# Layer 1 of a two-layer graph network: pairs of edge tiles, blocks of 42 nodes, and products of 126 or 128 rows and weight columns

## The chip, the cores and the metric

One core of one Trainium2 chip runs the whole program. The metric is the device time of one launch in microseconds (us), as the median of the runs shown. PE is TensorE's matrix unit, PEld its weight loads, DVE is VectorE, ACT is ScalarE, POOL is GpSimd, SP is SyncE.

## The reference, cut to what matters

There are 6250 nodes with 160 features (64 scalars, 32 vectors of 3) and 100,000 edges with `src` and `dst`; the edges are sorted by `dst`. Layer 0 passes messages and normalises; this change leaves its arithmetic alone. Layer 1 is:

```
h = relu(e10 @ W_fc1 / sqrt(10)) * sqrt(2);  w = h @ W_fc2 / 10      # per edge, 192 weights
y = node_linear(x)[src]                                               # per edge, 160 features
msg = (w0*y0, w1*y0) and (w2*y1, w3*y1), each times the four edge attributes a0..a3
agg = segment_sum(msg, dst)                                           # 16 edges a node on average
out = layernorm(x + self_part + a_node * (agg @ W_l2))
```

`a0` multiplies the scalar part and `a1..a3` are the components of the edge's direction: `w0*y0*a0` and `w2*y1*a0` keep their kind, `w1*y0*(a1,a2,a3)` makes a vector, and `w3*y1.(a1,a2,a3)` makes a scalar.

## The kernel before, in words

Phases follow one another with a barrier between them: setup, products, windows (which finds for every 32 nodes where their edges start, and tests that no block of nodes has more edges than its tiles hold), layer 0 with its nodes (up to about 2276 us), `layer1_edges` (from about 2280 to 3952 us) and `layer1_nodes` (the final scaling and the stores).

`layer1_edges` has a fast path, chosen at run time when the order of the edges and the size of the blocks allow it, and a slow path. All that follows is the fast path. A **block** is 32 nodes (`SUB`) with `TPB` = 5 tiles of 128 edges; 196 blocks make 980 tiles. A **group** is 4 blocks (128 nodes, 20 tiles, `BODY`); there are 49. The code is unrolled. Every engine has its own queue and runs a list of stages; a stage with lead L does at step s the work of tile s+L:

- SP loads the block's edge records (L1283), eight blocks ahead at most.
- POOL gathers the 128 rows of `y_table` for one tile by an indirect DMA into a ring of 16 (L1311). It waits until the tile 16 before it has been weighed.
- ACT issues three loads of `b_lengths` per block (L1535, four blocks ahead), rectifies the hidden layer in two halves (L1548, lead 14), copies the block's sums out of PSUM (L1555, lead 5) and the turned sums (L1560, L1561, lead 3).
- PE makes the hidden layer in two halves, in neighbouring steps and in one bank (L1454, lead 14), the 192 weights of a tile (L1461, lead 9, a ring of four banks), the sums of the block (L1468, lead 6: `f_hot` of 128 columns, 4 attributes by 32 nodes, as weights, `f_msg` of 320 columns moving), three transposes at the end of a block (L1477 to L1479, lead 4), and at the end of a group the 8 products with `w_post` (L1488 to L1494, lead 1).
- DVE makes the one-hot rows times the attributes (L1357, lead 9), the messages (L1372 and L1374, lead 8), the node numbers within a block (L1350) and at a group's end adds the node's own features and takes the moments (`finish`, L1385 to L1393, lead 0). A float32 product is two matmul instructions in the trace.

Not all of the products of 4 attributes with 320 columns are read. `p_trans` and `p_res` are one bank (`bank[1]`), so the first transposes of a group wait for `finish` (L1475), and `finish` waits for the group's last product:

```
p_bhid, p_trans, p_rad, p_acc, p_res = bank[0], bank[1], bank[2:6], bank[6:8], bank[1]
unrolled(pe, ALL, BODY, (14, hide), (9, radial), (6, add_up), (4, block_end(turn)), (1, group_end(combine)))
unrolled(dve, ALL, BODY, (9, select), (8, weigh), (0, group_end(finish)))
```

Of the kernel before, what the change touches and what calls it, by code (L numbers as in the profile page):

```python
# [26 lines left out]
TPB = 5  # L27
BLOCK_EDGES = TPB * P
HALF = BLOCK_EDGES // 2
SUB = 32  # L30
SUBS = P // SUB
TAIL = CHUNK * P
SMALL_BLOCKS = SUBS * FAST_BLOCKS
# [87 lines left out]
def build_program(nc, t, out):  # L121
    ctx = ExitStack()
    with ctx:
# [18 lines left out]
        v.y_table = dram("y_table", (FAST_BLOCKS * P, D))  # L142
        v.block_start = nc.dram_tensor("block_start", (2 * P, 1), I32).ap()
# [29 lines left out]
        v.w_post = sb("w_post", [P, 384])  # L173
# [15 lines left out]
        v.moments = sb("moments", [P, BLOCKS, 2])  # L189
# [7 lines left out]
        layer0(nc, t, v)  # L197
        layer1_edges(nc, t, v)
# [3 lines left out]
def setup_phase(nc, t, v):  # L202

    with ExitStack() as local:
# [24 lines left out]
        with nc.Block() as block:  # L229

            @block.sync
            def _(sp):
# [31 lines left out]
                load(v.w_post[S:P, 64:96], t["w_out1"][0:S, :])  # L264
                for i in range(3):
                    load(v.w_post[32 * i:32 * i + 32, 96 + 32 * i:128 + 32 * i], t["w_out1"][S:96, :])
                load(v.w_post[96:128, 192:256], t["w_out0"][S:96, :])
                load(v.w_post[0:32, 256:320], t["w_out0"][S:96, :])
                load(v.w_post[32:64, 320:384], t["w_out0"][S:96, :])
# [238 lines left out]
def windows_phase(nc, t, v):  # L508


    with ExitStack() as local:
# [46 lines left out]
        with nc.Block() as block:  # L558
# [32 lines left out]
            def _(dve):  # L591
# [56 lines left out]
                chain.link(dve.tensor_tensor(starts[:], full_tiles[:], inside[:], ALU.add))  # L648
                dve.tensor_copy(start_int[:], starts[:, 0:2]).then_inc(start_ready, 1)
# [38 lines left out]
def layer0(nc, t, v):  # L688
# [6 lines left out]
    with ExitStack() as local:  # L695
# [85 lines left out]
        with nc.Block() as block:  # L781

            def nodes_sync(sp, fast):
# [19 lines left out]
                def store(i, k):  # L803
                    sp.wait_ge(outs_ready, i * N + k + 3)
                    sp.dma_start(v.y_table[bass.ds((i * N + k) * P, P), :], y[k][:]).then_inc(stores[k], 16)

                def landed(i, k):
                    sp.wait_ge(stores[k], i * 16 + 16)
                    sp.sem_inc(stored, 1)
# [367 lines left out]
def layer1_edges(nc, t, v):  # L1177
# [6 lines left out]
    with ExitStack() as local:  # L1184
# [9 lines left out]
        R = 10  # L1194
        Y_RING = 16
        LENGTHS_RING = 4
        REC_RING = 8
        b_rec = [v.sb(f"b_rec{q}", [P, TPB, 6], I32, local) for q in range(REC_RING)]
        b_column = [v.sb(f"b_column{q}", [P, TPB], F32, local) for q in range(4)]
        b_lengths = [v.sb(f"b_lengths{q}", [96, BLOCK_EDGES], BF16, local) for q in range(LENGTHS_RING)]  # L1200
        b_hidden = [v.sb(f"b_hidden{q}", [100, TPB, P], F32, local) for q in range(2)]
        f_y = v.sb("f_y", [P, Y_RING, D], F32, local)
        f_hot = v.sb("f_hot", [P, R, 4, SUB], F32, local)
        f_msg = v.sb("f_msg", [P, R, MSG], F32, local)
        block_sums = [v.sb(f"block_sums{q}", [P, MSG], F32, local) for q in range(2)]
        sums_t = v.sb("sums_t", [P, 3, 4, SUBS, SUB], F32, local)
        block_whole = v.sb("block_whole", [P, D], F32, local)
        block_stats = v.sb("block_stats", [P, 8], F32, local)
# [9 lines left out]
        p_bhid, p_trans, p_rad, p_acc, p_res = bank[0], bank[1], bank[2:6], bank[6:8], bank[1]  # L1218
# [16 lines left out]
        rec_in, lengths_in = edges_in + [v.sem(f"e_rec_in{k}", local) for k in range(U, REC_RING)], scattered  # L1235
# [3 lines left out]
        passed_sp = v.sem("e_passed_sp", local)  # L1239
        prods, parts_dve, parts_act = weighed, end_dve, passed_dve  # L1240
# [10 lines left out]
        padded = zeroed  # L1251
        CLEARS = 16 * COPIES * (TABLE_ROWS // P // 3)
        STEPS = 5
        BODY = SUBS * TPB
        ALL = SMALL_BLOCKS * TPB

        def block_end(fn):

            def at(i, k):
                if k % TPB == TPB - 1:  # L1260
                    fn(i, k // TPB, i * SUBS + k // TPB)
            return at

        def group_end(fn):

            def at(i, k):
                if k == BODY - 1:
                    fn(i)
            return at

        with nc.Block() as block:

            def fast_sync(sp):
                sp.sem_inc(hid_full, 4)
                sp.sem_inc(weighed, BODY)

                def load_block(i, q):
# [3 lines left out]
                    if b >= REC_RING:  # L1281
                        sp.wait_ge(weighed, (b - REC_RING) * TPB + TPB + BODY)
# [503 lines left out]
```

## Time and profile before

| | us |
|---|---|
| median of 3 runs | 3978.24 (3974.26 to 3978.79) |
| the profiled execution, its own time | 3976.29 |
| its span, first to last instruction | 3974.6 |
| busy PE / PEld / DVE / ACT / POOL | 3159.4 / 2467.6 / 2079.3 / 773.7 / 1813.8 |
| mean granted TensorE clock | 0.923 of full speed |

Busy time is a sum over phases with different limits, and a matmul's end is modelled, so the stage has to be read by itself: the rows further down are of single stretches.

### The profile page before, as it was taken

To read this page: it belongs to the slowest core of one execution; us is meant where nothing else is said; L and a number is where in the kernel's file an instruction comes from. 1 tells how busy PE (TensorE), PEld (TensorE's weight loads), DVE (VectorE), ACT (ScalarE), POOL (GpSimd) and SP (SyncE) were. 2 spreads that over 40 slices of the span, in tenths; PEclk is the share of its full clock that TensorE was granted. 3 is DMA by queue.
4 is the path that set the end of the run, shared out by engine and by line. 5 is a ranking of instruction groups with operands and counts; after the bars stand their busy time and mean duration, and the time that the engine had idled before them with its cause. 6 is when DMAs were issued, how large, how long until landed. Compare 5 with 4: busy or idle time off the path is not lost. (4 is left out here: it accounts for less than half of the span.)

```text
span 3974.6 us, 61198 instructions
## 1 busy us (share of the span) xinstructions
PE 3159.4 (79%) x16014; PEld 2467.6 (62%) x16014; DVE 2079.3 (52%) x5812; ACT 773.7 (19%) x2531; POOL 1813.8 (46%) x2039
## 2 busy tenths in 40 slices
PE   0888838888888888887999867887878777777776
PEld 0333317777777777777888746665666556566664
DVE  3778864444444444444555545554555555555545
ACT  0333311111111111111111112221212122222111
POOL 1222215666666666662000065555555555555553
PEclk9999999999999999999999878888888888888888
DMA  7677758878887877874555332222222222222222
GB/s 287 283 316 307 313 192 230 228 227 231 228 230 227 231 227 229 231 224 174 196 203 200 117 72 64 67 63 66 63 64 66 63 65 66 65 67 67 63 63 77
DMA packets 493313, 641.02 MB, mean 161 GB/s; under 512 B 87161, under 2 KB 419541, under 8 KB 479782
## 3 DMA queue, kind: packets, MB, share of 16 engines
q1 hardware_dynamic: 130090, 308.44, 22.0%
q10 hardware_dynamic: 278124, 183.18, 16.8%
q0 software_dynamic: 84800, 145.68, 13.5%
q8 instruction: 155, 2.54, 0.3%
q14 instruction: 144, 1.17, 0.1%
HBM read 410.34 MB, written 226.72 MB: 160 GB/s over the span
## 5 line engine op out<-in xcount | busy, mean ns | idle before, releaser
L1311 POOL DMA_INDIRECT f_y<-y_table,b_rec x980 | 937.5, 957 | 1167.1 <-DMA b_rec<-in_records 461.4
L1087 PE MATMUL z_bank<-big,work 128*128 x6272 | 1008.9, 314 | 166.5 <-issue 101.2
L1087 PEld LDWEIGHTS z_bank<-big,work 128*128 128x128 f32 x6272 | 900.5, 196 | 274.3 <-issue 269.8
L855 POOL DMA_INDIRECT placed<-message,slots_now x784 | 762.8, 973 | 502.3 <-ACT message L1156 312.4
L963 DVE SCALAR_TENSOR_TENSOR work<-z_bank,quarter_node,work 128x512 f32<-128x512 f32 x784 | 534.2, 744 | 689.3 <-remote 333.0
L1468 PE MATMUL e_bank<-f_msg,f_hot 128*128 128x320 f32 x1960 | 786.4, 486 | 41.2 <-issue 26.7
L1372 DVE TENSOR_TENSOR f_msg<-e_bank,f_y 128x128 f32<-128x128 f32 x980 | 282.7, 289 | 626.1 <-PE e_bank L1461 329.8
L1461 PE MATMUL e_bank<-fc,b_hidden 100*128 100x192 f32 x1960 | 547.4, 364 | 0.0
L1461 PEld LDWEIGHTS e_bank<-fc,b_hidden 100*128 100x128 f32 x1960 | 399.5, 217 | 120.4 <-issue 36.6
L1468 PEld LDWEIGHTS e_bank<-f_msg,f_hot 128*128 128x128 f32 x1960 | 394.5, 215 | 53.3 <-issue 34.5
L1156 ACT COPY message<-z_bank 128x160 f32<-128x160 f32 x784 | 209.8, 296 | 946.0 <-PE z_bank L1087 720.1
L1374 DVE TENSOR_TENSOR f_msg<-e_bank,f_y 128x192 f32<-128x192 f32 x980 | 341.3, 348 | 0.3
L1357 DVE SCALAR_TENSOR_TENSOR f_hot<-count_row,b_column,b_rec 128x128 f32<-128x128 f32 x980 | 336.6, 344 | 0.0
L1548 ACT ACTIVATE b_hidden<-e_bank 100x320 f32<-100x320 f32 x392 | 171.5, 437 | 817.4 <-remote 342.3
L1454 PE MATMUL e_bank<-b_lengths,fc_parts 96*100 96x320 bf16 x392 | 135.4, 345 | 222.3 <-issue 110.4
L1005 PE MATMUL z_bank<-big,work 128*128 128x161 f32 x1764 | 259.5, 306 | 16.0 <-DVE work L904 16.0
L1005 PEld LDWEIGHTS z_bank<-big,work 128*128 128x128 f32 x1764 | 248.1, 193 | 19.4 <-issue 16.4
L1454 PEld LDWEIGHTS e_bank<-b_lengths,fc_parts 96*100 96x100 bf16 x392 | 53.6, 137 | 293.0 <-issue 140.7
L401 POOL TENSOR_TENSOR r_ties<-r_ties,earlier 128x256 f32<-128x256 f32 x50 | 36.3, 726 | 324.8 <-DVE r_ties L487 324.8
L1555 ACT COPY block_sums<-e_bank 128x320 f32<-128x320 f32 x196 | 83.5, 426 | 517.9 <-PE e_bank L1468 359.6
L438 PE MATMUL g_bank<-w,xs 64*128 64x512 f32 x100 | 103.6, 1138 | 63.9 <-DMA xv<-in_x_t 63.9
L1477 PE MATMUL e_bank<-ident,block_sums 128*128 128x128 f32 x196 | 59.9, 306 | 109.6 <-ACT block_sums L1555 49.6
(217 smaller groups left out, 2771.6 us busy)
## 6 DMA issues: line engine op xcount, KB each, us to landing
big<-products ACTq DMA_DIRECT2D x49, 3200.0 KB
products<-g SPq DMA_DIRECT2D x50, 2560.0 KB, 7.5
big<-placed SPq DMA_DIRECT2D x49, 1458.0 KB, 6.8
work<-in_e_t SPq DMA_DIRECT2D x784, 64.0 KB
b_lengths<-length_parts ACTq DMA_DIRECT2D x588, 37.5 KB
placed<-zeros SPq DMA_DIRECT2D x1, 15876.0 KB, 49.9
f_y<-y_table,b_rec POOLq DMA_INDIRECT x980
placed<-message,slots_now POOLq DMA_INDIRECT x784
```

The costliest lines, as they stand in the source:

```text
L855: pool.indirect_dma_start(v.placed[:, :], bass.IndirectOffsetOnAxis(slots_now[tile // SET % SLOT_SETS][:, tile % SET:tile % SET + 1], 0), ...
L963: last = dve.scalar_tensor_tensor(spread[h % 2][:, j, :], p_node[h % 2][:], v.quarter_node[:, j:j + 1], features[h].rearrange("p a b -> p ...
L1005: last = pe.matmul(p_agg[k % 2], hot[k % 2][:, j, :], placed_rows[k][:, j, 0:MW], start=(j == 0), stop=(j == ROWS - 1))
L1087: last = pe.matmul(p_msg[q][:, 0:D], spread[h % 2][:, j, q * P:q * P + P], windows[:, bass.ds(slot + j, 1), :].rearrange("p a b -> p (a b) ...
L1156: act.copy(message[:, k % TILE_RING, 0:D], p_msg[q][:, 0:D]).then_inc(copied, 1)
L1311: pool.indirect_dma_start(f_y[:, tile % Y_RING, :], None, v.y_table[:, :], bass.IndirectOffsetOnAxis(b_rec[b % REC_RING][:, j, 0:1], 0)).t ...
L1357: dve.scalar_tensor_tensor(f_hot[:, r, :, :], v.count_row[:, 0:SUB].unsqueeze(1).broadcast_to([P, 4, SUB]), b_column[q][:, j:j + 1], b_rec ...
L1372: dve.tensor_tensor(f_msg[:, r, 0:128].rearrange("p (g c) -> p g c", g=2), w[:, 0:128].rearrange("p (g c) -> p g c", g=2), f_y[:, tile % Y ...
L1374: dve.tensor_tensor(f_msg[:, r, 128:320].rearrange("p (g i c) -> p g i c", g=2, i=3), w[:, 128:192].rearrange("p (g c) -> p g c", g=2).uns ...
L1454: pe.matmul(p_bhid[0:100, 0:HALF], v.fc1_parts[:], b_lengths[b % LENGTHS_RING][:, c * HALF:(c + 1) * HALF], start=True, stop=True).then_in ...
L1461: pe.matmul(p_rad[k % 4][:, 0:192], b_hidden[q % 2][:, j, :], v.fc2[:], start=True, stop=True).then_inc(rad_full, 1)
L1468: pe.matmul(p_acc[q % 2][:, 0:MSG], f_hot[:, r, :, :].rearrange("p s n -> p (s n)"), f_msg[:, r, :], start=(j == 0), stop=(j == TPB - 1)). ...
```

## The change

Tiles are worked on in pairs; the stages' leads now count pairs. A block is 42 nodes with 6 tiles (3 pairs, 768 edges), a group is 3 blocks (126 nodes). There are 149 blocks, 894 tiles, 447 pairs and 50 groups. A tile's sums are now two products: `level` takes attributes 0 to 2 (126 weight columns) with the 160 columns that keep their kind, `turned` takes attributes 1 to 3 with the other 160. `w_post` has 128 rows in every slice, with zeros in the rows that don't count. The transposes multiply by a rotated identity, so that the third part of the sums stands first or last. `p_res` has a bank of its own; `p_rad` has three banks with a pair in each. DVE makes the 64-column part of two tiles' messages in one instruction. Since groups are 126 nodes and layer 0's blocks 128, layer 0 also stores the node's own features to DRAM (`own_table`) and layer 1 loads them back by groups of 126.

```diff
-TPB = 5                      +TPB = 6
-SUB = 32                     +SUB = 42
-SUBS = P // SUB              +SUBS = 3; GROUP = SUBS * SUB; GROUPS = -(-NODES // GROUP)
-SMALL_BLOCKS = SUBS * FAST_BLOCKS
+SMALL_BLOCKS = -(-NODES // SUB)
 # windows_phase
+chain.link(dve.tensor_scalar(starts[:], starts[:], float(EDGES), None, ALU.min))
 # layer 0, store
-sp.dma_start(v.y_table[bass.ds((i * N + k) * P, P), :], y[k][:]).then_inc(stores[k], 16)
+sp.dma_start(v.y_table[at, :], y[k][:]).then_inc(stores[k], 16)
+sp.dma_start(v.own_table[at, :], v.own[:, bass.ds(i * N + k, 1), :].rearrange("p a d -> p (a d)")).then_inc(stores[k], 16)
 # layer1_edges
-R = 10; LENGTHS_RING = 4; b_hidden x 2
+R = 12; LENGTHS_RING = 6; HIDDEN_RING = 3; BPP = TPB // 2; BODY = SUBS * BPP; ALL = SMALL_BLOCKS * BPP
-p_bhid, p_trans, p_rad, p_acc, p_res = bank[0], bank[1], bank[2:6], bank[6:8], bank[1]
+p_bhid, p_trans, p_res, p_rad, p_acc = bank[0], bank[1], bank[2], bank[3:6], bank[6:8]
 # SP: eight record loads, then grouped (4 DMAs, own_in), then the other record loads
+sp.dma_start(v.grouped[:, 0:GROUPS - 1, :], v.own_table[0:(GROUPS - 1) * GROUP, :].rearrange("(g p) d -> p g d", p=GROUP)).then_inc(own_in, 16)
 # POOL, gather
-pool.wait_ge(weighed, tile - Y_RING + 1 + BODY)
+if pair >= Y_RING // 2:
+    pool.wait_ge(weighed, pair - Y_RING // 2 + 1)
+for n in range(2):
+    tile, j = 2 * pair + n, 2 * (pair % BPP) + n
     pool.indirect_dma_start(f_y[:, tile % Y_RING, :], ...)
 # DVE, weigh
+dve.tensor_tensor(f_msg[:, r:r + 2, :, 0:S], w[:, :, 0:128].rearrange("p t (g c) -> p t g c", g=2),
+                  f_y[:, at:at + 2, 0:S].unsqueeze(2).broadcast_to([P, 2, 2, S]), ALU.mult)
+for n in range(2):
+    last = dve.tensor_tensor(f_msg[:, r + n, :, S:D]..., w[:, n, 128:192]..., f_y[:, at + n, S:D]..., ALU.mult)
 # PE, radial: two tiles into one bank, after the pair three before has been weighed
+if pair >= 3:
+    pe.wait_ge(weighed, pair - 2)
+for n in range(2):
+    last = pe.matmul(p_rad[pair % 3][:, 192 * n:192 * n + 192], b_hidden[b % HIDDEN_RING][:, 2 * (pair % BPP) + n, :], v.fc2[:], start=True, stop=True)
 # PE, add_up
-pe.matmul(p_acc[q % 2][:, 0:MSG], f_hot[:, r, :, :]..., f_msg[:, r, :], start=(j == 0), stop=(j == TPB - 1)).then_inc(added, 1)
+def turned(j): return pe.matmul(p_acc[b % 2][0:3 * SUB, D:MSG], f_hot[:, r, 1:4, :]..., f_msg[:, r, 1, :], ...)
+def level(j):  return pe.matmul(p_acc[b % 2][0:3 * SUB, 0:D], f_hot[:, r, 0:3, :]..., f_msg[:, r, 0, :], start=False, stop=False)
+level(j); turned(j); level(j + 1); turned(j + 1).then_inc(added, 1)
 # PE, turn: no wait for end_dve; four transposes
+pe.transpose(p_trans[:, 0:GROUP], level[:, 0:128], level_last[:])
+pe.transpose(p_trans[:, GROUP:2 * GROUP], turned[:, 0:128], v.ident[0:GROUP, 0:GROUP])
+pe.transpose(p_trans[:, 2 * GROUP:3 * GROUP], level[:, V:D], level_last[:])
+pe.transpose(p_trans[:, 3 * GROUP:4 * GROUP], turned[:, V:D], third_first[:]).then_inc(sums_turned, 1)
 # PE, combine: six products of 128 rows and 126 weight columns, 128, 96, 128, 32, 32 and 64 columns moving
-unrolled(pe, ALL, BODY, (14, hide), (9, radial), (6, add_up), (4, block_end(turn)), (1, group_end(combine)))
+unrolled(pe, ALL, BODY, (14, hide(0)), (10, radial), (8, add_up), (14, hide(1)), (6, block_end(turn)), (3, group_end(combine)))
-unrolled(act, ALL, BODY, (14, rectify), (5, block_end(take_sums)), (3, block_end(take_turned)))
+unrolled(act, ALL, BODY, (14, rectify(0)), (8, block_end(take_sums)), (14, rectify(1)), (6, block_end(take_turned)))
 # layer1_nodes: 50 groups of 126 rows in place of 49 blocks of 128; six stores in place of five
```

DVE's stages keep their leads (9, 8 and 0), now in pairs. The columns of the hidden layer's halves go from 320 to 384.

## Rows read from the trace of the kernel before

**Rows 1.** Windows: bounds, length, busy by engine, granted clock, DMA share, GB/s.

```profile
500.00:1700.00 1200.00, 984.10 (x5926) 842.06 (x5921) 543.71 (x924) 215.72 (x906) 697.35 (x732) 0.97 0.77 225
...
2350.00:3850.00 1500.00, 1178.47 (x5152) 913.85 (x5152) 773.35 (x3115) 304.75 (x889) 849.43 (x888) 0.86 0.27 65
```

**Rows 2.** The gathers' line: count, duration min/median/max in ns, first and last start.

```profile
L1311 POOL DMA_INDIRECT f_y<-y_table,b_rec x980: 943/949/1082, 2284.2 to 3926.4; - x196
```

**Rows 3.** Waits in 2300 to 3900 us: total us, times, longest.

```profile
POOL f_y L1311 <- DVE f_msg L1374: 437.7, 290, 5.9
...
DVE f_msg L1372 <- PE e_bank L1461: 322.5, 234, 4.9
...
DVE block_whole L1385 <- PE e_bank L1494: 98.6, 32, 3.9
...
DVE block_whole L1385 <- remote: 54.3, 12, 5.9
```

**Rows 4.** POOL in order of time: start, duration, instruction, [idle before].

```profile
2449.31 0.94 POOL L1311 DMA_INDIRECT f_y<-y_table,b_rec  x1 [0.30 <-issue]
2454.35 0.94 POOL L1311 DMA_INDIRECT f_y<-y_table,b_rec  x1 [4.10 <-DVE f_msg L1374]
```

**Rows 5.** POOL in order of time, four gathers issued without a wait.

```profile
555.50 0.94 POOL L587 DMA_INDIRECT edge_nodes<-in_dst_rows,edge_tile  x1 [0.30 <-issue]
```

**Rows 6.** PE in order of time, a group's end in layer 1.

```profile
2443.06 0.30 PE L1454 MATMUL e_bank<-b_lengths,fc_parts 96*100 96x320 bf16 x1
2443.20 0.49 PE L1461 MATMUL e_bank<-fc,b_hidden 100*128 100x192 f32 x2
...
2445.07 0.49 PE L1461 MATMUL e_bank<-fc,b_hidden 100*128 100x192 f32 x2
2445.40 0.70 PE L1468 MATMUL e_bank<-f_msg,f_hot 128*128 128x320 f32 x2
2445.94 0.33 PE L1488 MATMUL e_bank<-w_post,sums_t 128*128 128x64 f32 x2
...
2447.59 0.38 PE L1494 MATMUL e_bank<-w_post,sums_t 64*128 64x64 f32 x2
2447.90 0.59 PE L1461 MATMUL e_bank<-fc,b_hidden 100*128 100x192 f32 x2
...
2452.35 0.30 PE L1477 MATMUL e_bank<-ident,block_sums 128*128 128x128 f32 x1 [2.45 <-DVE block_whole L1386]
```

**Rows 7.** DVE in order of time, the same group's end.

```profile
2451.55 0.28 DVE L1385 SCALAR_TENSOR_TENSOR block_whole<-e_bank,a_col,own 128x64 f32<-128x64 f32 x1 [5.08 <-remote]
...
2453.27 0.35 DVE L1357 SCALAR_TENSOR_TENSOR f_hot<-count_row,b_column,b_rec 128x128 f32<-128x128 f32 x1
2453.53 0.28 DVE L1372 TENSOR_TENSOR f_msg<-e_bank,f_y 128x128 f32<-128x128 f32 x1
2453.74 0.35 DVE L1374 TENSOR_TENSOR f_msg<-e_bank,f_y 128x192 f32<-128x192 f32 x1
```

**Rows 8.** PE in order of time, layer 0's nodes.

```profile
2036.86 5.21 PE L1005 MATMUL z_bank<-big,work 128*128 128x161 f32 x36
2041.90 0.27 PE L1016 MATMUL z_bank<-ident,agg 128*128 128x128 f32 x1
```

**Rows 9.** PE in order of time, a stretch at the lower clock.

```profile
2468.82 0.85 PE L1461 MATMUL e_bank<-fc,b_hidden 100*128 100x192 f32 x2
2469.45 1.27 PE L1468 MATMUL e_bank<-f_msg,f_hot 128*128 128x320 f32 x2
```

**Rows 10.** ACT in order of time, the start of layer 1.

```profile
2283.18 9.61 ACTq L1535 DMA_DIRECT2D b_lengths<-length_parts  x12
```

**Rows 11.** PE in order of time, the last sums.

```profile
3944.08 1.78 PE L1468 MATMUL e_bank<-f_msg,f_hot 128*128 128x320 f32 x6
```

**Rows 12.** DVE in order of time, the program's end.

```profile
3951.41 0.17 DVE L1393 COPY moments<-block_stats 128x2 f32<-128x2 f32 x1
...
3954.04 13.47 DVE L1708 TENSOR_SCALAR own<-own,moments,f_scale 128x160 f32<-128x160 f32 x49
```

More of the change, by code:

```diff
@@ L1239, in layer1_edges @@
         passed_sp = v.sem("e_passed_sp", local)
+        rec_in, lengths_in = edges_in + [v.sem(f"e_rec_in{k}", local) for k in range(U, REC_RING)], scattered + [passed, passed_sp]
         prods, parts_dve, parts_act = weighed, end_dve, passed_dve
@@ L1384, in finish @@
+                    dve.wait_ge(combined, i + 1)
                     whole = block_whole[:, S:D].rearrange("p (c i) -> p i c", i=3)
-                    chain.step(dve.scalar_tensor_tensor(block_whole[:, 0:S], p_res[:, 0:S], a, own[:, 0:S], ALU.mult, ALU.add))
-                    chain.link(dve.scalar_tensor_tensor(whole, p_res[:, S:D].rearrange("p (i c) -> p i c", i=3), a, vectors, ALU.mult, ALU.add))
+                    chain.step(dve.scalar_tensor_tensor(block_whole[:, 0:S], p_res[0:GROUP, 0:S], a, own[:, 0:S], ALU.mult, ALU.add))
@@ L1387, in finish @@
+                    chain.link(dve.scalar_tensor_tensor(whole, p_res[0:GROUP, S:D].rearrange("p (i c) -> p i c", i=3), a, vectors, ALU.mult, ALU.add))
                     dve.sem_inc(passed_dve, 1)
@@ new lines, in radial @@
+                def radial(i, k):
+                    pair = i * BODY + k
+                    b = pair // BPP
+                    if pair % BPP == 0:
+                        pe.wait_ge(hid_done, b * 2 + 2)
+                    if pair >= 3:
+                        pe.wait_ge(weighed, pair - 2)
+                    for n in range(2):
+                        last = pe.matmul(p_rad[pair % 3][:, 192 * n:192 * n + 192], b_hidden[b % HIDDEN_RING][:, 2 * (pair % BPP) + n, :], v.fc2[:], start=True, stop=True)
+                    last.then_inc(rad_full, 1)
@@ new lines, in add_up, with turned, level @@
+                def add_up(i, k):
+                    pair = i * BODY + k
+                    b = pair // BPP
+                    if pair % BPP == 0 and b >= 2:
+                        pe.wait_ge(sums_taken, b - 1)
+                    pe.wait_ge(weighed, pair + 1)
+                    def turned(j):
+                        r = (b * TPB + j) % R
+                        return pe.matmul(p_acc[b % 2][0:3 * SUB, D:MSG], f_hot[:, r, 1:4, :].rearrange("p s n -> p (s n)"), f_msg[:, r, 1, :],
+                                         start=(j == 0), stop=(j == TPB - 1))
+                    def level(j):
+                        r = (b * TPB + j) % R
+                        return pe.matmul(p_acc[b % 2][0:3 * SUB, 0:D], f_hot[:, r, 0:3, :].rearrange("p s n -> p (s n)"), f_msg[:, r, 0, :], start=False, stop=False)
+                    j = 2 * (pair % BPP)
+                    if j == 0:
+                        turned(j)
+                        level(j)
+                    else:
+                        level(j)
+                        turned(j)
+                    level(j + 1)
+                    turned(j + 1).then_inc(added, 1)
```

284 lines of the change are left out of this document (149 added, 135 removed).

## The prediction

> **What bounds the kernel now.** I began with the busy time by stretches [rows 1]. In layer 1 (2350 to 3850 us) no engine is full: PE 1178 of 1500 us, DVE 773, POOL 849, at a granted clock of 0.86; layer 0 has 984 of 1200 us on PE at 0.97. So layer 1 waits for something that isn't an engine's capacity, and loses clock on top.
>
> Next the gathers. There are 980 from 2284.2 to 3926.4 us, one in 1.68 us on average [rows 2]. One takes 0.95 us, and the next never starts sooner than 0.30 us after it, even where nothing is waited for [rows 5]: a pitch of 1.25 us, 980 of which are 1225 us. The other 438 us POOL waited for DVE's messages [rows 3], so that its ring of 16 was full; POOL isn't what is late.
>
> Then who keeps DVE: the message instruction waited 323 us for TensorE's weights, and `finish` 99 + 54 us for the group's last product [rows 3]. The group's end shows how [rows 6, 7]. The last product starts at 2447.59 us, DVE takes it up only at 2451.55 us (some 3.6 us after its modelled end), the transposes wait for that until 2452.35 us, since they share a bank with `p_res`, and POOL stands until 2454.35 us [rows 4]. PE has nothing to do for 2.45 us, and later rows show the lower clock, where a tile's weights and the step to its sums take 0.63 us in place of 0.33 us [rows 6, 9].
>
> The stage from the first gather to the last moments, 2284.2 to 3951.58 us [rows 2, 12], is 1667.4 us: 8.51 us a block of 5 tiles, 1.70 us a tile. The last gather's start to that end is 25.2 us, because 16 gathers are ahead.
>
> **The change, part by part.**
>
> *Gathers.* 894 in place of 980, 86 fewer. At a pitch of 1.254 us (median duration 0.949 plus 0.30, rounded up) [rows 2, 5] they need 1121 us. The pitch holds without waits too, so that waiting once a pair saves nothing. From below the pitch is 0.943 + 0.30 = 1.243 us (1111 us), from above 1.082 + 0.30 = 1.38 us (1235 us); I take the median.
>
> *TensorE, at full clock.* Two instructions of a tile's weights take 0.33 us from start to start, two of its sums with 320 columns 0.54 us [rows 6]. New: the sums are four instructions of 160 columns. The nearest row is layer 0's 161 columns with a weight load each, 36 from 2036.86 to 2041.90 us, 0.140 us each [rows 8]. So a pair is 2 x 0.33 + 8 x 0.140 = 1.78 us, against 1.74 us for two tiles before: twice the weight loads cost 0.04 us. A block has 3 pairs (5.34), two hidden halves (0.14 us at 320 columns [rows 6], 0.17 at 384: 0.34), four transposes at no more than 0.14 each (0.56), and a third of 12 product instructions (before 16 in 1.96 us, 0.12 each [rows 6]: 0.49). That is 6.73 us, and 1003 us for 149 blocks. By the same rows the old block is 5 x 0.87 + 0.28 + 0.42 + 0.49 = 5.54 us, 1086 us in all.
>
> *VectorE.* In a run without waits a tile costs 0.26 us to the next start for the one-hot, 0.21 for the 64-column part, and about 0.26 for the other [rows 7], 0.73 us. L1374 has 64 elements more than L1372 and lasts 0.35 against 0.28 us, so 64 elements are 0.07 us. In the new pair the two one-hots have 168 in place of 128 elements (0.30 each), the joint part 256 (0.35), the two others 0.26 each: about 1.5 us of the 2.51 us in which a pair is gathered. With node numbers and `finish` (1.9 us a group, from 2451.55 to the next one-hot at 2453.27 and some) that is under 17 of 22.6 us a group. DVE is covered.
>
> *Gathers now outlast TensorE.* A block's six gathers take 7.52 us, its TensorE work 6.73 us. Before, POOL needed 6.27 us and TensorE 5.54 us, so the order was the same; what lost the time was the handshakes. They go: `combine` runs three pairs ahead of `finish`, before the weights of the pair that DVE needs to get there, so that `finish` finds it done; the turn doesn't wait for `end_dve`; the two hidden halves are a pair apart instead of a tile; each lead in pairs is about twice as long in time, and DVE may lag 8 pairs (20 us) before POOL stops. The next thing that is late is the gather itself. A pair's loop (weights, message, weights three pairs on) has 3 x 2.51 = 7.5 us for its 1.5 us of DVE work, so a completion that comes 3.6 us late fits inside it.
>
> *The clock.* With PE at work 6.73 of 7.52 us (0.89), more than in layer 0's stretch, I expect a granted clock near its 0.97. From below the cost is nothing; from above the whole stage keeps 0.86 (next part).
>
> *The start.* ACT issues 18 length loads before it rectifies, not 12: 9.61 us becomes 14.4 [rows 10], and the first message comes 4.8 us later. POOL has 16 gathers (20 us) to issue meanwhile, so it doesn't stop; without that cover it would be 4.8 us. SP's four loads of `grouped` (4 MB) stand behind the first eight record loads, which reach to the 48th gather, 60 us on; the first `finish` is 16 pairs on, 40 us. Hidden; if they compete with the gathers, a few us once.
>
> *The end.* Last gather's start: 2284.2 + 893 x 1.254 = 3404.0 us. Then landing, message, sums, turn, products, `finish`: no less than 0.95 + 0.9 + 1.1 + 5.7 (from the end of the last sums, 3945.86, to 3951.58 us [rows 11, 12]) = 8.7 us, no more than the 25.2 us of before; I take 12, since nothing is backed up. That is 3416.0 us. Then 2.5 us to the scaling, 13.47 x 50/49 = 13.7 us of it, and 7.1 us from its end (3967.51) to the span's end at 3974.6 us: 3439.3 us.
>
> *Elsewhere.* Layer 0 issues 49 more stores of 80 KB beside a PE that is full there; the last one and one more step in the windows phase: 2 us. For gaps that aren't explained by any wait (0.01 us a gather) I add 9 us, from 0 to the upper pitch above. Span 3450 us; the profiled execution stood 1.7 us over its span, so 3452 us, a gain of 524 us on 3976.29 us. The median of the runs stood 2 us above that execution: **3454 us**.
>
> *A rule that speaks against it.* Layer 0's 36 instructions with a weight load each start every 0.140 us, and 161 columns in two clocks each are 0.134 us at 2.4 GHz, so the load is hidden [rows 8]. The Trainium skill (TensorE: Matmul & The Clock Gate, "The mechanism") says that a weight load overlaps a matmul in flight only where the row groups differ, and its section on LDWEIGHTS puts a load at columns / 1.2 ns, 107 ns for 128; by an estimate from that page the twelve more loads of a block would cost 1.3 us, and TensorE would be the longer engine. That rule would be rival C; the trace contradicts it for these shapes.
>
> **The rivals.**
>
> A, the forecast: bound by the gathers, 3435 to 3500 us.
>
> B: TensorE stays late. Its completions keep coming late as in [rows 6, 7], the clock stays at 0.86, and TensorE, not POOL, is the bound: 1003 / 0.86 = 1166 us, plus about 1 us a block of waits as are left (149) = 1315 us against 1121: 3454 + 194 = 3650 us; with half of that loss 3550 us. For it: the late completions aren't explained by anything in the trace, and TensorE's spare is only 0.8 us in 7.5. Against: the loop has room, and the stall that cost most is gone.
>
> C: the added weight loads aren't hidden. 24 x (0.140 + 0.125) for the sums of a block instead of 3.36 is 3.0 us more, 9.7 us a block, 1450 us: 3783 us. Against: [rows 8].
>
> D: the waits go with the tile, whatever the order of the stages: 1.70 x 894 = 1521 us, 146 less than before: 3830 us. Against: the shared bank and the leads are seen in the rows.
>
> E, slower: TensorE sinks to the lower clock for the stage. At 1.2 GHz its 1003 us double; with a share s of the work there it takes 1003 x (1 + s), and passes the old 1667 us at s = 0.66. With all of it: 2006 us, 340 us slower, 4316 us. For it: more and shorter matmuls, and 0.86 now. Against: PE idles less than before.
>
> That the change doesn't do what it says: a block that held over 768 edges would send everything down the slow path. The `dst` of the inputs puts 733 in the fullest block of 42 nodes, so the fast path holds.
>
> **How the numbers follow.** A 0.58, B 0.28, C 0.04, D 0.06, E 0.02, the rest 0.02. The time is A's. A begins at 3432 us (no stray gaps, tail at its lower bound), and to leave out no more than 2 in 10 the range goes through most of B: 3432 to 3630 us. A difference from no change can be told from 0.2% on, the width of the three runs being 0.11%. Faster by over 0.2%: A to D, 0.96; within it 0.01; slower 0.03.
>
> **What would show it.** Right: gathers start every 1.25 us nearly throughout, with almost no wait for DVE; `finish` and the transposes wait for nothing; DVE's message waits for gathers to land; granted clock of the stage over 0.93. The sums' instructions start every 0.14 us. Wrong: POOL still waits for hundreds of us (B or D); sums 0.25 us apart (C); a clock under 0.7 (E).

## The result and the profile after

| | kernel before | changed kernel |
|---|---|---|
| median of four runs each | 3978.51 us | 3761.73 us (3759.92 to 3768.43) |
| ratio | | 0.9459 (0.9443 to 0.9475) |
| profiled execution, its span | 3976.29, 3974.6 us | 3760.95, 3759.1 us |
| gathers, first to last start | 980, 1642.2 us | 894, 1423.6 us |

The change gained 217 us; I had forecast 524 us (3454 us, range 3432 to 3630), so the time lies outside the range. The gathers' line of the changed kernel, which answers to [rows 2]:

```profile
L1341 POOL DMA_INDIRECT f_y<-y_table,b_rec x894: 940/946/1106, 2285.3 to 3708.9; - x179
```

It starts 1.1 us after the 2284.2 us that I had, and its last gather starts 305 us after my 3404.0 us: 1.594 us a gather, not 1.254. The windows, which answer to [rows 1] (bounds, length, PE, PEld, DVE, ACT, POOL busy, granted clock, DMA share, GB/s):

```profile
500.00:1700.00 1200.00, 976.52 (x5925) 829.32 (x5920) 543.57 (x925) 215.87 (x905) 695.38 (x731) 0.98 0.78 225
2350.00:3650.00 1300.00, 1021.81 (x6232) 966.50 (x6233) 700.04 (x2441) 233.63 (x678) 776.64 (x815) 0.90 0.28 69
```

No engine is full and the granted clock is 0.90. An engine tells the others by a semaphore that a piece of work is done; I call that its report. The waits between 2290 and 3700 us, which answer to [rows 3]; "remote" stands where no record of another engine ended at the time at which the semaphore came:

```profile
ACT b_hidden L1600 <- remote: 464.9, 68, 11.6
DVE f_msg L1402 <- remote: 365.4, 74, 6.6
POOL f_y L1341 <- DVE f_msg L1405: 311.4, 105, 4.1
...
DVE f_msg L1402 <- PE e_bank L1499: 213.5, 90, 7.1
```

`finish` and the transposes are no longer among them: in [rows 3] `finish` alone had 153 us, now L1419 waited 5.4 us in two places. What is left is mostly one thing: VectorE and ScalarE wait for products of TensorE that its records show as done, and POOL then waits for VectorE. (The end of a TensorE record is modelled, its start is not; whether the product or only the report is late, the trace doesn't tell.) One such stall in order of time, all engines (start, duration, instruction, [idle before]):

```profile
2999.76 0.33 PE L1488 MATMUL e_bank<-b_lengths,fc_parts 96*100 96x384 bf16 x1
...
3000.36 0.82 PE L1499 MATMUL e_bank<-fc,b_hidden 100*128 100x192 f32 x4
...
3002.64 0.95 POOL L1341 DMA_INDIRECT f_y<-y_table,b_rec  x1 [0.30 <-issue]
3003.04 0.42 DVE L1402 TENSOR_TENSOR f_msg<-e_bank,f_y 128x256 f32<-128x256 f32 x1 [2.85 <-remote]
...
3005.14 0.95 POOL L1341 DMA_INDIRECT f_y<-y_table,b_rec  x1 [0.31 <-issue]
3006.39 0.95 POOL L1341 DMA_INDIRECT f_y<-y_table,b_rec  x1 [0.30 <-issue]
3008.63 0.49 ACT L1600 ACTIVATE b_hidden<-e_bank 100x384 f32<-100x384 f32 x1 [11.50 <-remote]
...
3009.27 0.53 PE L1488 MATMUL e_bank<-b_lengths,fc_parts 96*100 96x384 bf16 x1 [7.01 <-issue]
...
3009.53 0.42 DVE L1402 TENSOR_TENSOR f_msg<-e_bank,f_y 128x256 f32<-128x256 f32 x1 [4.94 <-remote]
3009.59 1.48 PE L1499 MATMUL e_bank<-fc,b_hidden 100*128 100x192 f32 x4
...
3011.26 0.94 POOL L1341 DMA_INDIRECT f_y<-y_table,b_rec  x1 [3.93 <-DVE f_msg L1405]
```

The hidden product is on record at 2999.76 us and the weights of a pair at 3000.36. ScalarE takes the first at 3008.63 us. Counted from the first pair on, the message at 3003.04 us belongs to weights of 2998.02 us, and that at 3009.53 us to those of 3000.36, 8.4 us after their end. Meanwhile POOL issues a gather every 1.25 us until its ring is full, the last at 3006.39 us. Only then these two products are taken, 0.9 us apart; TensorE has stood 7.01 us and works at the lower clock after it (four radial instructions in 1.48 us, not 0.82).

### The profile page after: what moved, and what is told of

Read it like the earlier page. It is cut to its first block and busy times, and to the rows that moved or that the text cites. A ratio compares the mean times of both kernels' runs of the same rounds, so it can differ in the third digit from the quotient of the medians.

```text
span 3759.1 us, 60760 instructions
## 1 busy us (share of the span) xinstructions
PE 2972.5 (79%) x17188; PEld 2508.1 (67%) x17188; DVE 1997.1 (53%) x5074; ACT 694.3 (18%) x2296; POOL 1726.9 (46%) x1953
## 5 line engine op out<-in xcount | busy, mean ns | idle before, releaser
L1341 POOL DMA_INDIRECT f_y<-y_table,b_rec x894 | 852.5, 954 | 1034.9 <-DMA b_rec<-in_records 462.8
L1098 PE MATMUL z_bank<-big,work 128*128 x6272 | 1000.0, 311 | 177.1 <-issue 117.2
L1098 PEld LDWEIGHTS z_bank<-big,work 128*128 128x128 f32 x6272 | 886.6, 193 | 290.1 <-issue 285.4
L866 POOL DMA_INDIRECT placed<-message,slots_now x784 | 761.0, 971 | 503.5 <-ACT message L1167 310.4
L1402 DVE TENSOR_TENSOR f_msg<-e_bank,f_y 128x256 f32<-128x256 f32 x447 | 186.7, 418 | 650.7 <-remote 374.3
L1516 PE MATMUL e_bank<-f_msg,f_hot 128*126 128x160 f32 x1788 | 414.6, 327 | 64.2 <-issue 51.0
L1511 PE MATMUL e_bank<-f_msg,f_hot 128*126 128x160 f32 x1788 | 423.2, 319 | 31.5 <-issue 31.5
L1499 PE MATMUL e_bank<-fc,b_hidden 100*128 100x192 f32 x1788 | 418.3, 361 | 0.0
L1516 PEld LDWEIGHTS e_bank<-f_msg,f_hot 128*126 128x126 f32 x1788 | 320.2, 208 | 89.6 <-issue 68.3
L1511 PEld LDWEIGHTS e_bank<-f_msg,f_hot 128*126 128x126 f32 x1788 | 325.0, 205 | 36.0 <-issue 35.9
L1499 PEld LDWEIGHTS e_bank<-fc,b_hidden 100*128 100x128 f32 x1788 | 340.0, 216 | 1.2
L1390 DVE SCALAR_TENSOR_TENSOR f_hot<-count_row,b_column,b_rec 128x168 f32<-128x168 f32 x894 | 311.7, 389 | 0.0
L1488 PE MATMUL e_bank<-b_lengths,fc_parts 96*100 96x384 bf16 x298 | 108.4, 364 | 236.3 <-ACT b_hidden L1600 198.3
L1600 ACT ACTIVATE b_hidden<-e_bank 100x384 f32<-100x384 f32 x298 | 148.0, 497 | 744.8 <-remote 476.8
L1405 DVE TENSOR_TENSOR f_msg<-e_bank,f_y 128x192 f32<-128x192 f32 x894 | 272.3, 345 | 0.0
L1016 PE MATMUL z_bank<-big,work 128*128 128x161 f32 x1764 | 259.9, 306 | 15.0 <-DVE work L915 15.0
L1016 PEld LDWEIGHTS z_bank<-big,work 128*128 128x128 f32 x1764 | 248.5, 193 | 18.3 <-issue 15.4
```

Of the source, the lines that this page charges most:

```text
L866: pool.indirect_dma_start(v.placed[:, :], bass.IndirectOffsetOnAxis(slots_now[tile // SET % SLOT_SETS][:, tile % SET:tile % SET + 1], 0), ...
L1016: last = pe.matmul(p_agg[k % 2], hot[k % 2][:, j, :], placed_rows[k][:, j, 0:MW], start=(j == 0), stop=(j == ROWS - 1))
L1098: last = pe.matmul(p_msg[q][:, 0:D], spread[h % 2][:, j, q * P:q * P + P], windows[:, bass.ds(slot + j, 1), :].rearrange("p a b -> p (a b) ...
L1341: pool.indirect_dma_start(f_y[:, tile % Y_RING, :], None, v.y_table[:, :], bass.IndirectOffsetOnAxis(b_rec[b % REC_RING][:, j, 0:1], 0)).t ...
L1390: dve.scalar_tensor_tensor(f_hot[:, r, :, :], v.count_row[:, 0:SUB].unsqueeze(1).broadcast_to([P, 4, SUB]), b_column[b % COLUMNS][:, j:j + 1],
L1402: dve.tensor_tensor(f_msg[:, r:r + 2, :, 0:S], w[:, :, 0:128].rearrange("p t (g c) -> p t g c", g=2), f_y[:, at:at + 2, 0:S].unsqueeze(2). ...
```

## Experiments

Kernels told of together ran on one chip beside the kernel before. That was needed: **the kernel before itself took 3979 to 3981 us on two of the chips, as in the result, and 3331 to 3338 us on three others**. I call these the late and the prompt condition; the forecast's profile and the result are of the late one. Each of the five chips was used once, so what belongs to the chip and what to the hour isn't separated. A time is compared only within its condition.

### First set: hidden product, gathers, transposes, handshake (prompt, kernel before 3333.56 us)

`full_hidden`: zeros up to 128 rows and columns.

```
-pe.matmul(p_bhid[0:100, 0:HALF], v.fc1_parts[:], b_lengths...)   # [96, 100]
+pe.matmul(p_bhid[:, 0:HALF], fc1_full[:], b_lengths...)          # [128, 128]
-... b_hidden[...][:, ..., :], v.fc2[:]                           # 100 rows
+... b_hidden[...][:, ..., :], fc2_full[:]                        # 128 rows
```

> The changed kernel with the hidden product brought to 128 contraction rows and 128 weight columns (they were 96 and 100) and the radial product to 128 rows (they were 100), zeros filled in; the output is the same. Three theories of why layer 1 took 1.62 us a tile where 1.254 (POOL's gathers) was forecast. H1, the products that don't fill the array make TensorE report its completions late: with all of them full the late reports go, the stage falls to about 894 x 1.26 = 1126 us and the time to 3440 to 3520. H2, the gathers' landings hold the reports back: nothing changes, 3745 to 3775. H3, the single bank of the hidden product and its handshake with ScalarE set the pace: nothing changes either, 3745 to 3775. I hold H1 for possible, not likely (0.25).

`half_gathers`: in `gather`, `for n in range(1)` in place of `range(2)`, and the same in VectorE's wait for the gathers; the second tile's rows are zeros.

> The changed kernel with the gather of every second tile left out (its rows of y are a constant, so the output isn't the reference's); the products, messages and all waits among the other engines stay. If the gathers' pitch (1.25 us on POOL) or their transfers set the stage (H2), POOL needs 447 x 1.25 = 559 us and the stage falls to what TensorE's products take, 149 x 6.73 = 1003 us, and the idle time of VectorE behind the radial product (579 us of idle time before L1402) falls below 150: 3300 to 3380 in all. If TensorE's late reports and its handshake with ScalarE set it (H1, H3), the stage stays above 1300 us: 3600 to 3765.

`no_turns`: one product of 8 columns for four transposes, and one of 160 for the six of `combine`.

> The changed kernel with the four transposes of a block replaced by one product of 8 columns, its copies by one of 8 columns, and the six products of a group by one of 160 columns (left out of the computation: turning the sums and most of the output product). If the transposes or the switching among kinds of product cause the late reports, these go and the stage becomes the gathers' 1126 us: 3440 to 3520. If TensorE's amount of work counts, 149 x (4 x about 0.2 + 2.0/3) = about 200 us of TensorE's time go, and some of it shows: 3560 to 3700. If neither, 3740 to 3765.

`late_rectify`: leads only.

```
-PE  (14, hide(0)), ... (14, hide(1))      ACT (14, rectify(0)), (8, take_sums), (14, rectify(1))
+PE  (15, hide(0)), ... (14, hide(1))      ACT (14, rectify(0)), (13, rectify(1)), (8, take_sums)
```

> The changed kernel with slack in the handshake of the hidden product: TensorE issues the first half's product one pair of tiles earlier (lead 15 for 14) and ScalarE takes the second half one pair later (lead 13 for 14), so that a report that comes up to one pair (2.5 us) late holds up nobody. If the handshake is what turns late reports into loss (H3), most of ScalarE's 465 us of waits for the product and TensorE's 191 us behind ScalarE go, and the time falls by 100 us or more: 3450 to 3660. If the reports' lateness is spent elsewhere (radial product to VectorE), 3730 to 3770.

Measured: 3239.12, 3083.97, 3237.51 and 3245.10 us. The three with all gathers agree within 8 us, and their gathers are 1.27 us apart (full_hidden: 2068.0 to 3200.9 us for 894). All four miss their ranges, which were written for the late condition, and none of the theories could be told from another, because the late reports weren't there in any of the four. What half_gathers gives is TensorE's own pace: 447 pairs from 2092.6 to 3046.0 us, 2.138 us a pair, 6.41 us a block.

### Second set: both kernels unaltered (prompt, before 3337.74 us)

> The changed kernel, unaltered, run again beside the one before, since in the first four experiments the kernel before took 3333 us where it had taken 3978 us. Theory T1: what cost my forecast its 308 us is a condition of the chip in which TensorE reports its products late, and which wasn't there in those experiments; the change itself does what I worked out (stage = 894 gathers x 1.25 us). Then, where the kernel before takes about 3333 us, the changed one takes 3230 to 3260 with the gathers 1.25 us apart through the stage and the granted clock above .97; where the kernel before takes about 3978, it takes about 3760. Rival T2: the changed kernel has waits of its own that the four variants happened to take away each in its way; then it takes over 3300 beside 3333.

> The kernel before, unaltered, for its profile in the same condition. T1 where it takes about 3333 us: layer 1's stage, 3926 - 2284 = 1642 us in the first profile, is 1210 to 1260 us here, VectorE's idle time behind the radial product falls from several hundred us to under 150, and the gathers, 980 of them, stand 1.25 us apart (980 x 1.25 = 1225 us). Rival: the stage is still above 1400 us and the saving is all in layer 0.

Measured: changed 3242.81 us, ratio 0.9722 (0.9706 to 0.9739); earlier 3338.33 us. Theory T1 stands. The gathers' line of the changed kernel, then its waits between 2070 and 3190 us, then the line of the kernel before:

```profile
L1341 POOL DMA_INDIRECT f_y<-y_table,b_rec x894: 942/946/1167, 2067.9 to 3199.4; - x179
```

```profile
DVE f_msg L1402 <- issue: 247.0, 277, 1.8
...
POOL f_y L1341 <- DVE f_msg L1405: 105.4, 335, 3.1
...
DVE f_msg L1402 <- DMA f_y<-y_table,b_rec: 44.9, 46, 2.1
...
DVE f_msg L1402 <- PE e_bank L1499: 35.3, 18, 20.1
```

```profile
L1311 POOL DMA_INDIRECT f_y<-y_table,b_rec x980: 945/949/1082, 2069.5 to 3300.0; - x196
```

No "remote" wait is left in layer 1 in either kernel (975 us of them in the changed kernel's late profile, on engines that wait at the same time). The gathers take 1131.5 us and 1230.5 us, 1.267 and 1.257 us each: in this condition both kernels are bound by POOL's pitch, and the change gains about what 86 gathers fewer are worth (108 us at 1.257 us each, less 9 us because the pitch is 0.01 us longer): 99 us in this stage and 95 us in all.

The two profiles also show where lateness lives. Layer 0 scatters through POOL in one stage (L866) and then sums with TensorE alone (L1016), no POOL DMA beside it. Late condition (after), then prompt (changed):

```profile
L866 POOL DMA_INDIRECT placed<-message,slots_now x784: 965/971/1007, 603.3 to 1821.5; - x196
```

```profile
L1016 PE MATMUL z_bank<-big,work x1764: 297/299/607, 1833.2 to 2256.5; 128*128 128x161 f32 x196
```

```profile
L866 POOL DMA_INDIRECT placed<-message,slots_now x784: 965/971/1005, 603.5 to 1602.7; - x196
```

```profile
L1016 PE MATMUL z_bank<-big,work x1764: 297/299/607, 1614.6 to 2036.1; 128*128 128x161 f32 x196
```

The stage with POOL's DMAs takes 1218.2 us late and 999.2 us prompt; the stage without them 423.3 and 421.5 us, the same, though TensorE is full in it (400 of 400 us from 1850 to 2250 in the late profile). So layer 0 loses 219 us in the late condition too, in both kernels; that is not in the change's account. No run leaves POOL's DMAs out of layer 0, and they aren't the stages' only difference. The theory that small products bring lateness (H1) isn't settled by these rows: ScalarE waits there 127.2 us of "remote" for products of 128 x 128 (L1098), but a product of one row (L1084) stands among them. The fourth set says more.

### Third set: reports made late on purpose (late, before 3980.61 us)

`late_radial` and `later_radial` (and `earlier_late_radial` by two tiles):

```
-dve.wait_ge(rad_full, pair + 1)
+dve.wait_ge(rad_full, min(pair + 2, ALL))   # later_radial: pair + 3
```

`late_all` adds, before ScalarE's rectify, `act.wait_ge(rad_full, pair - 2)`.

> The changed kernel, in which VectorE takes the radial product of a pair only once TensorE has reported the product of the next pair: an imitation of reports that come late by one pair, about 2.5 us. It asks whether the loop of a pair has the slack that I forecast (three banks, 7.5 us). If it has: the loop over two pairs is messages 1.0 + sums 1.1 + radial 0.8 + two reports of 0.3 = 3.5 us where two pairs of gathers take 5.0, so the stage stays at the gathers' pace, within 10 us of the unaltered 3243. If one pair of lateness is already too much: 3300 to 3500.

> The same, two pairs late. Now the loop closes in one pair: 3.5 us against the gathers' 2.5. If the loop is as I think, the stage is 447 x 3.5 = 1565 us and the time about 3650 to 3700, and POOL's waits are for the messages; if the three banks give less slack than I think, more; if the report costs nothing here, 3243.

> As late_radial, and besides ScalarE takes the hidden product only once a radial product issued about a pair after it has been reported, so both of the waits in which the slow profile has its long gaps (VectorE's for the radial product, ScalarE's for the hidden product) are late by about a pair. If the handshake over the single bank of the hidden product is what turns late reports into loss: its loop is product, report, rectify, product, twice a block, so 2 x (2.5 + 0.5 + 0.5) = 7 us of a block's 7.5, on the edge: 3260 to 3400. If it has slack: 3240 to 3255.

> The kernel before, with the radial product taken two tiles late, the same 2.5 us, against four banks of one tile each. If the rings of the two kernels have about the same slack, it stays at 3338. If the earlier ring has less, 3380 to 3600, and a part of the larger ratio under late reports (0.946 for 0.972) is explained by the pairs' deeper ring.

Measured: 3785.05, 3937.58, 3815.03 and 3930.93 us. The expectations were written for the prompt condition and the chip was in the late one, so on the ring's slack the set is inconclusive: taking the weights one pair later costs the changed kernel 23 us (against 3761.73 in the result, on another chip), and the kernel before even gains 50 us (ratio 0.9876), which I can't explain. The lesson is later_radial. Its line and window:

```profile
L1341 POOL DMA_INDIRECT f_y<-y_table,b_rec x894: 940/944/1097, 2280.9 to 3879.6; - x179
```

```profile
2350.00:3650.00 1300.00, 871.12 (x5577) 761.96 (x5578) 645.17 (x2180) 210.69 (x607) 686.20 (x727) 1.00 0.25 61
```

The stage is 1598.7 us, 3.58 us a pair where I worked out 3.5 for the closed loop, at a granted clock of 1.00, without one "remote" wait. TensorE and POOL both stand still in every pair here, and no report of layer 1 is late, on a chip in the late condition, though layer 0 of the same run has 460 us of "remote" waits. So it isn't simply TensorE that is slow there, and it isn't the number of gathers: all 894 are issued, 1.79 us apart on average and nearly always two in a row, where the late profile has 4.8 in a row on average, up to 16.

### Fourth set: the gathers themselves (late, before 3979.22 us)

`no_gathers`: POOL does nothing. `half_gathers_late`: as above. `plain_loads`, on SyncE:

```
+for pair in range(ALL):
+    ...
+    sp.dma_start(f_y[:, at:at + 2, :], v.y_table[row:row + 2 * P, :]...).then_inc(y_in[at], 16)
```

> The changed kernel with all of layer 1's gathers left out (y is zero, so the output isn't the reference's). G1, POOL's indirect DMAs bring the late reports out: where the kernel before takes about 3980, the stage loses nothing any more and becomes TensorE's: 149 x 6.6 = 983 us, so about 3762 - 1424 + 983 = 3320. G2, the lateness belongs to TensorE's own load (its products are denser without the gathers' pace): 3400 to 3750. Where the kernel before takes about 3338: 3060 to 3095 by both.

> The kernel half_gathers again (every second tile's gather left out), for the condition in which the kernel before takes about 3980. G1 with a loss by the gather: 292 / 2 = 146 us of loss on the TensorE-bound 980, so 3762 - 1424 + 1126 = 3465. G2: within 30 us of no_gathers. Where the kernel before takes about 3338: 3084 again.

> The changed kernel with each pair's two gathers replaced by one direct load of as many rows of y from SyncE's queue (other rows, so the output isn't the reference's): the same bytes, no indirect DMA and no work of POOL. If it is POOL's way of making the transfers that brings the lateness out, it equals no_gathers to 20 us. If the traffic or its landings do, it equals the unaltered kernel's loss: 3550 to 3765 where the kernel before takes 3980. Where that takes about 3338: 3060 to 3100.

> The kernel no_turns again (a block's four transposes are one product of 8 columns, a group's six products one), for the condition in which the kernel before takes about 3980. The loss was 412 us over 196 blocks before and 292 over 149 after, 2.1 and 2.0 us a block: if it comes with a block's transposes, it goes here: 3470 to 3520. If it comes with the gathers or TensorE's load in general: 3650 to 3760. Where the kernel before takes about 3338: 3237 again.

Measured: 3299.24, 3301.44, 3301.88 and 3745.00 us. One row of each of the first three: VectorE's message line without gathers, the window of plain_loads, the gathers' line with half of them:

```profile
L1401 DVE TENSOR_TENSOR f_msg<-e_bank,f_y x447: 414/424/426, 2307.3 to 3260.2; 128x256 f32<-128x256 f32 x149
```

```profile
2350.00:3200.00 850.00, 850.00 (x6085) 844.01 (x6085) 683.18 (x2382) 221.43 (x664) 0.00 (x0) 1.00 0.40 103
```

```profile
L1341 POOL DMA_INDIRECT f_y<-y_table,b_rec x447: 943/947/1160, 2285.5 to 3246.7; - x149
```

Without gathers a pair takes (3260.2 - 2307.3) / 446 = 2.137 us, to a nanosecond what it took in the prompt condition. TensorE is busy 850 of 850 us (2350 to 3200 us) at a clock of 1.00 in all three, denser than in the late profile (668 of 850), and not late: G2 falls. So does H1, at least by itself, since the hidden product of 96 x 100 and the weights' product of 100 rows are all still there. Loading the same bytes through SyncE (103 GB/s, against 69 in the late profile) brings no lateness either, so it isn't the amount of traffic. G1 is right as to what, wrong as to how much: I expected half the loss with half the gathers, 3465 us, and there is none in layer 1. The three still take some 215 us more than half_gathers in the prompt condition: that is layer 0's loss, which stays. Leaving out the transposes and products takes away no more than 17 us of the 292, which is not clear of the noise (ratio 0.9407, 0.9351 to 0.9463, beside the result's 0.9459): lateness doesn't come with a block's transposes, though 412 us over 196 blocks and 292 over 149 had looked so.

Counted from the semaphores in the trace of the changed kernel (each report set against the last product of its kind that had ended before it): of all reports of TensorE in the stage, 598 came over 1 us late. 383 of them came between 2.5 and 3.25 us after the last gather's start, and none later than 3.5 us after it. For the weights alone 113 reports of 403 came over 2 us late, 105 of them while POOL had stopped (over 1.3 us after the last gather's start), and it is stopped so for 21% of the time. POOL stops because messages are late, so a part of this follows from the ring; I see nothing in the ring that would give the narrow spacing after the last gather. In the prompt profile POOL issues 81 gathers in a row on average, and each of the 425 reports of the weights is on record within 0.02 us of its product's modelled end.

### Fifth set: where lateness begins (prompt, before 3331.19 us)

`five_gathers`, `four_gathers`: the gathers of tile 5, or 3 and 5 (counted from 0), of a block left out. `paced_gathers`, `slower_gathers`: after each gather

```
+if tile:
+    pool.wait_ge(pace_done, tile)
+pool.memset(pace[:, 0:16], 0.0).then_inc(pace_done, 1)   # slower_gathers: 0:256
```

> The changed kernel with the gather of each block's sixth tile left out (y of an older tile stands in, so the output isn't the reference's): 745 gathers x 1.254 = 934 us, just under TensorE's 953 us in no_gathers. P1, the reports come late only where POOL's gathers set the pace and are issued back to back: the stage is TensorE's, and where the kernel before takes 3980 it takes 3300 to 3350. P2, the lateness grows with their rate: (745 - 447) / (894 - 447) = 2/3 of the way from half_gathers_late to the unaltered kernel's loss, about 3500 to 3620. Where the kernel before takes 3338: 3070 to 3110.

> The same with four gathers of six: 596 x 1.254 = 747 us of POOL. P1: 3300, as half_gathers_late. P2: a third of the way, 3380 to 3460. Where the kernel before takes 3338: 3084.

> The changed kernel with a small clear (16 elements) on POOL after every gather, each waiting for the one before; all gathers and the output stay. It puts some 0.1 to 0.2 us between two gathers: 894 x 1.4 = 1250 us if nothing else sets the stage. P3, a break between the DMA instructions is enough to let the reports through: where the kernel before takes 3980, 2285 + 1250 + 50 = about 3590, which beats the changed kernel's 3762. If no: 3740 to 3850. Where the kernel before takes 3338: 3243 + 90 to 180.

> The same with a clear of 256 elements, some 0.35 us a gather, so 1.6 us from gather to gather, the mean pace that the unaltered kernel has in the late condition: 894 x 1.6 = 1430 us. With P3 or with a rate as the cause the reports are prompt and the pace is even: 3760 to 3780, no 'remote' waits in the profile. If lateness has nothing to do with the pace, it adds to it: 3850 to 4100. Where the kernel before takes 3338: 3540 to 3560.

Measured: 3088.41, 3085.83, 3248.83 and 3403.15 us. The chip was in the prompt condition, so P1 to P3 stay open, and paced_gathers wasn't tried where it might help. What the set does show is the crossing of the two bounds: with five gathers of six POOL's 934 us lie under TensorE's 953, and the time is already that of four or three. And POOL's row of paced_gathers:

```profile
2500.56 0.13 POOL L1347 MEMSET pace<- 128x16 f32 x1
2500.87 0.95 POOL L1343 DMA_INDIRECT f_y<-y_table,b_rec  x1 [0.18 <-issue]
```

The clear of 16 elements hides in the 0.30 us that always lies between two gathers (1.276 us a gather on average, against 1.267 unaltered; 8 us in the stage). With 256 elements it takes 0.33 us, but the gathers are 1.449 us apart on average, not the 1.6 that I added up. I expected 0.1 to 0.2 us a gather from the first (3333 to 3423 us) and 3540 to 3560 us from the second; both were wrong, for the same reason. No version with all gathers beat the changed kernel by more than the noise.

## Why the prediction was wrong

**The steps that held.** *Gathers:* where reports are prompt, the changed kernel needs 1131.5 us for my 1120 (1.267 for 1.254 us). *From first gather to the span's end* I had 3450 - 2284.2 = 1165.8 us; the prompt profile has 3236.7 - 2067.9 = 1168.8. That near a match is luck in part: the pitch was 0.013 us too low (12 us in all), and the 9 us of stray gaps paid for it. *TensorE:* 6.73 us a block forecast, 6.41 measured. *Weight loads hidden:* rival C is false, by the rows below: two instructions of 160 columns, each with its own weight load, every 0.27 us. *Handshakes of the group's end:* gone. *The end:* 35.3 us from the last gather, 37.3 prompt, 50.2 late.

```profile
3001.01 0.44 PE L1516 MATMUL e_bank<-f_msg,f_hot 128*126 128x160 f32 x2
3001.15 0.32 PEld L1511 LDWEIGHTS e_bank<-f_msg,f_hot 128*126 128x126 f32 x2
3001.28 0.43 PE L1511 MATMUL e_bank<-f_msg,f_hot 128*126 128x160 f32 x2
...
3001.55 0.43 PE L1516 MATMUL e_bank<-f_msg,f_hot 128*126 128x160 f32 x2
```

The rule of the Trainium skill that I weighed (TensorE: Matmul & The Clock Gate, "The mechanism"), that a weight load overlaps a matmul in flight only where their row groups differ, doesn't fit these rows: each of the loads has all 128 rows. The same section also lets a load go ahead of matmuls in flight when it goes into the background weight buffer, which I had passed over and which these rows don't contradict.

*The start* was wrong by a little. I wrote that the first message would come 4.8 us later and that POOL wouldn't stop. The message comes 21.6 us after the first gather, where the kernel before had 11.6 us, and POOL stops at the 17th gather, 3.04 us late and 3.10 us prompt. Kernel before, then changed kernel:

```profile
2295.74 0.29 DVE L1372 TENSOR_TENSOR f_msg<-e_bank,f_y 128x128 f32<-128x128 f32 x1 [10.91 <-issue]
```

```profile
2306.91 0.42 DVE L1402 TENSOR_TENSOR f_msg<-e_bank,f_y 128x256 f32<-128x256 f32 x1 [20.10 <-issue]
...
2308.13 0.94 POOL L1341 DMA_INDIRECT f_y<-y_table,b_rec  x1 [3.04 <-DVE f_msg L1405]
```

**The step that failed** is "a completion that comes 3.6 us late fits inside it", and with it "the clock near 0.97". I took the lateness of [rows 6, 7] for a fixed 3.6 us, of the size seen there, and asked if a pair's loop of 7.5 us has room for that. So the sum had nothing for it. In the late profile such a product is taken up to 9.2 us after its end (the hidden product recorded at 3691.26 us, taken at 3700.75), and VectorE idles up to 6.6 us and ScalarE up to 11.6 us before it takes one. Many of these waits end only once POOL's ring of 16 is full; my reading, not shown, is that more room in the loop is filled with gathers issued, not with work. The stage lost 292 us to it (1423.6 - 1131.5), where the kernel before lost 412 us (1642.2 - 1230.5): 0.33 us a gather, not 0.42, and not nothing. The clock was 0.90 for it, not 0.97. The rest of the 308 us is small: the end is 15 us longer (50.2 for 35.3), the pitch takes 12 us more, and the 9 us of stray gaps and 2 us of layer 0 that I added come off.

So of 217 us gained, some 95 are the fewer gathers, as the prompt runs show, and some 120 are lateness that the changed kernel doesn't suffer. Which part of the change spares it (deeper ring in time, 447 reports of weights in place of 980, the turned waits) no run tells.

**The rivals.** B had the right cause, late completions that persist, but I priced it as TensorE bound at a lower clock (3650 us, 3550 with half); TensorE is not the bound (79% busy over 2350 to 3650 us); the late reports are, and POOL stops behind them. D, waits by the tile at 1.70 us, gave 3830 us; measured 1.59 us a tile. Both together had 0.34, and the range's end at 3630 us lay below B's own full price of 3650 us and left out all between it and D. Its lower end isn't my sum either: without stray gaps and with the shortest end the sum is 3442 us, and 3432 takes the lower pitch (1111 us) as well.

**What was in the profile.** [rows 1] to [rows 9] show the lateness unexplained, and I gave 0.58 to its going away. The rows to look for were those of the stage that didn't suffer: L1005 of the kernel before ran TensorE full (180 of 180 us from 1850 to 2030) and between 2040 and 2270 us has no wait of this kind, while layer 0's scatter stage, which I took for healthy at a clock of 0.97, has 449 us of "remote" waits. One difference between that stage and the two that suffered is POOL's indirect DMAs, which the change keeps, 894 of 980.

**What stays open.** Why the reports are held in one condition and not in the other, and whether that is a matter of the chip. Also whether a rate of gathers or their being issued without a break sets it off: half_gathers_late (2.16 us a gather, 1.4 in a row on average) and later_radial (1.79 us, 2.0 in a row) are prompt in layer 1, the two kernels with 4.0 and 4.8 in a row are late, and both theories fit that. It was not tried at five or four gathers, nor paced, in the late condition. The loss in layer 0 wasn't tested by any run.

## What to carry to other kernels

A wait that the profile shows but doesn't explain is a term of the sum, at its present size per unit of what goes beside it, until a stage of the same trace without it shows what removes it. Look for the stage where the same engine works as densely and is not late, and ask what runs beside it in the others. Run the kernel before beside every experiment: here the same program took 16% less on one chip than on another, and the change's worth differed by a factor of over two (217 and 95 us).

## What the runs showed of the hardware

- Beside back-to-back indirect DMAs of POOL (pitch 1.25 us), on two of five chips and on that of the result, products that TensorE's records show as done are taken by other engines up to 9.2 us later, mostly once POOL stops. With half as many indirect DMAs in layer 1, none, or the same bytes on SyncE's queue, there is no such wait in layer 1 and the whole program takes 3299 to 3302 us, not 3762. With all of them, but two in a row and then a stop (later_radial), there is none either.
- In that condition some instructions of TensorE's own sequencer take longer too: of its 3136 register instructions beside layer 0's products 101 last over 100 ns, and none in the prompt condition. Late (after) and prompt (changed), in ns min/median/max:

```profile
L1098 PEldq FUSED_REGOPS  x3136: 2/55/1276, 599.5 to 1817.4; - x196
```

```profile
L1098 PEldq FUSED_REGOPS  x3136: 51/55/65, 599.7 to 1591.5; - x196
```

- The granted clock follows: 0.90 over 2350 to 3650 us late, 1.00 in later_radial, where TensorE is busy for less of the time (871 of 1300 us) but has no long stop.
